# Attention scores from two-part fp32r operands on the array's two row halves, in place of three-part bf16 operands on 96 rows

## What is computed

```
q, k, v = split(x @ w)                      # layer 0: 32 heads of k and v; layer 1: 8, each for 4 heads of q
q, k = rope(q), rope(k)                     # 16 features a head
scores = q @ k^T / sqrt(16), causal         # 1024 x 1024 for each of 32 heads
attn = softmax(scores) ; y = attn @ v
```

## Time and profile before

| | us |
|---|---|
| median of 3 runs (1092.49 to 1099.5) | 1098.1 |
| span of the profiled execution | 1084.4 |
| PE busy, of it | 924.4 |
| DVE busy | 700.9 |
| ACT busy | 485.7 |
| POOL busy | 254.2 |
| mean granted TensorE clock, of full speed | 0.917 |

### The profile page before, as it was taken

One profiled execution on the slowest core, in us unless ns is written; L12 is line 12 of the kernel. 1 busy time (PEld: TensorE's weight loads), 2 busy tenths in 40 slices (PEclk: granted clock), 3 DMA queues, 4 the chain that ended last, 5 costly groups with the idle time before them and its releaser, 6 DMA issues. The chain is left out here.

```text
span 1084.4 us, 17334 instructions
## 1 busy us (share of the span) xinstructions
PE 924.4 (85%) x5462; PEld 512.0 (47%) x5462; DVE 700.9 (65%) x1305; ACT 485.7 (45%) x750; POOL 254.2 (23%) x397
## 2 busy tenths in 40 slices
PE   7879943789988898888977877999999988799998
PEld 5557821333333333257535532333444426677766
DVE  6975332668666766448584765988888835745564
ACT  4221401336544655642262213566666673346730
POOL 2554020022112111210614531221212223012300
PEclk9998965889889989999788977999999999999999
DMA  9221161112211321020001330011111101042001
GB/s 315 88 89 59 23 144 42 42 48 87 71 56 59 81 72 54 11 97 1 1 0 56 103 94 23 24 46 46 46 44 44 24 1 39 11 173 78 20 21 59
DMA packets 45537, 64.87 MB, mean 60 GB/s; under 512 B 9056, under 2 KB 32160, under 8 KB 43936
## 3 DMA queue, kind: packets, MB, share of 16 engines
q1 hardware_dynamic: 45472, 64.01, 19.7%
HBM read 51.27 MB, written 12.32 MB: 59 GB/s over the span
## 5 line engine op out<-in xcount | busy, mean ns | idle before, releaser
L1035 DVE TENSOR_REDUCE mx<-psum 128x1 f32<-128x512 f32 (+3 forms) x640 | 372.1, 632 | 157.9 <-PE psum L866 132.1
L980 ACT ACTIVATE arena_p<-psum 128x1024 f32<-128x1024 f32 (+3 forms) x384 | 294.0, 808 | 271.5 <-PE psum L883 270.7
L861 PE MATMUL psum<-arena_s 96*128 96x512 bf16 (+3 forms) x768 | 236.7, 349 | 53.8 <-DMA arena_s<-k_parts 43.4
L883 PE MATMUL psum<-arena_s 99*128 99x512 bf16 (+3 forms) x768 | 191.1, 340 | 30.3 <-DMA arena_s<-mT 26.7
L1098 POOL TENSOR_SCALAR_AFFINE_SELECT arena_p<-arena_p 128x256 f32<-128x256 f32 x256 | 102.8, 407 | 472.5 <-ACT arena_p L980 470.7
L903 PE MATMUL psum<-arena_p,v_grp 128*32 128x512 f32 (+3 forms) x1536 | 171.2, 519 | 2.1 <-POOL arena_p L1098 1.9
L861 PEld LDWEIGHTS psum<-arena_s 96*128 96x128 bf16 x768 | 77.5, 102 | 200.9 <-DVE mx L1035 107.4
L883 PEld LDWEIGHTS psum<-arena_s 99*128 99x128 bf16 x768 | 64.9, 100 | 94.9 <-ACT arena_p L980 23.4
L866 PE MATMUL psum<-maskb,ident_b 128*128 128x128 bf16 x512 | 109.1, 235 | 0.0
L255 PE MATMUL psum<-x_h,w 128*128 128x512 f32 x224 | 89.9, 465 | 10.4 <-DVE w L472 7.3
L866 PEld LDWEIGHTS psum<-maskb,ident_b 128*128 128x128 bf16 x512 | 54.1, 106 | 13.0 <-issue 1.6
(11 more groups left out here) (200 smaller groups left out, 1087.3 us busy)
## 6 DMA issues: line engine op xcount, KB each, us to landing
q_parts<-arena_p SPq DMA_DIRECT2D x48, 128.0 KB
arena_s<-q_parts SPq DMA_DIRECT2D x32, 192.0 KB, 3.0
arena_s<-k_parts SPq DMA_DIRECT2D x16, 384.0 KB
ff_raw<-in_w_in SPq DMA_DIRECT2D x11, 512.0 KB, 3.5
arena_s<-q_parts SPq DMA_DIRECT2D x32, 128.0 KB, 2.9
arena_s<-k_parts SPq DMA_DIRECT2D x16, 256.0 KB
k_parts<-arena_p SPq DMA_DIRECT2D x30, 128.0 KB
arena_w<-in_w SPq DMA_DIRECT2D x12, 256.0 KB, 6.5
```

Of the source, the lines that this page charges most:

```text
L861: last = pe.matmul(psum[:, bank, width * n:width * n + width], q_st[0:KS, s, c, 512 * r + P * i:512 * r + P * i + P], k_max[0:KS, s, T * k ...
L883: last = pe.matmul(psum[:, 2 * hp + h, o:512], k_exp[0:KM, s, T * kh + P * kt:T * kh + P * kt + P], q_st[0:KM, s, c, 512 * r + o:512 * r + ...
L980: act.activation(pr[:, n % NP_RING, :, o:512], psum[:, 2 * (b % 2):2 * (b % 2) + 2, o:512], ACT.Exp, scale=scale).then_inc(exp_ready, 1)
L1035: dve.tensor_reduce(mx[:, kc, col:col + 4 * len(heads) - 3:4], src, AX, ALU.max)\
```

## The change

q and k become two parts each in fp32r (4 bytes an element): high and the rest. q is stored as high, high, low and k as high, low, high, so one head's three products take 48 rows, with two rows of the maximum (50). Heads r = 0, 2 of a group lie on partitions 0 to 49, heads 1, 3 on 64 to 113, and two heads' scores are issued next to each other on the two row halves. One k buffer serves both jobs. Its constant -1 rows are in DRAM, stored once by SP in layer 0's projection.

The units run chunk by chunk: all eight short ones, then all eight long ones. The max pieces run two units ahead in place of one group. Buffers for q and k are four units deep, the first four units' loads are issued ahead (layer 0) or the first one's (layer 1). The maxima are split in two by POOL (`split_max`), and turned in fp32. The causal mask is two small bf16 matmuls on 64 rows, 128 and 64 columns wide, in place of one of 128. All loops are written out. In the projection POOL's and DVE's middle steps fall away, the parts have twice the bytes, and the order of units changes to chunk by chunk.

```diff
-
-PAIRS = [(0, 0), (1, 0), (2, 0), (0, 1), (1, 1), (0, 2)]
-KS = len(PAIRS) * D
-KM = KS + NPART
+KS = NPART * D
+KM = KS + 2
+NS = 4
 VW = 32
 ADP = 10
...
+    for c in range(CH):
+        both = [[("q", t, c) for t in range(KC)], [("k", t, c) for t in range(nk)]]
+        units += both[layer] + both[1 - layer]
 
...
+                                 parts[:, n % 2, part, :].bitcast(F32)).then_inc(stored[n % 2], 16)
+                if layer == 0 and n == 0:
+                    sp.wait_ge(consts, 7)
+                    for k_dst in m["k_parts"]:
+                        heads = k_dst.shape[0]
+                        for c in range(CH):
+                            sp.dma_start(k_dst[:, KS:KM, 512 * c:512 * c + 512], minus[0:2 * heads, :])\
+                                .then_inc(minus_stored, 16)
...
-                dve.wait_ge(mid_ready, n + 1)
-                dve.tensor_tensor(parts[:, n % 2, 2, :], t_cos[:, n % 2, :], parts[:, n % 2, 1, :],
+                dve.wait_ge(hi_ready, n + 1)
+                if n >= 2:
+                    dve.wait_ge(stored[n % 2], 16 * NPART * (n // 2))
+                dve.tensor_tensor(parts[:, n % 2, 1, :], rotated(n), parts[:, n % 2, 0, :].bitcast(F32),
                                   ALU.subtract).then_inc(lo_ready, 1)
 
             def cut_low(n):
...
-                pool.wait_ge(hi_ready, n + 1)
-                pool.tensor_tensor(t_cos[:, s, :], rotated(n), parts[:, s, 0, :], ALU.subtract)\
-                    .then_inc(res_ready, 1)
 
...
-
-
-    kr, q_st, k_max, k_exp = stacked.kr, stacked.q, stacked.k_max, stacked.k_exp
-    q_loaded, km_loaded, ke_loaded = stacked.q_loaded, stacked.km_loaded, stacked.ke_loaded
+    def load(self, sp, u):
+
+        c, g = divmod(u, NG)
+        s, n = u % NS, 512 * (c + 1)
+        for t in range(2):
+            sp.dma_start(self.q[64 * t:64 * t + KS, s, :, :].bitcast(F32),
+                         self.q_parts[g, t, :, :, 512 * c:n]).then_inc(self.q_loaded[s], 16)
+            if self.layer == 0:
...
-                sp.wait_ge(qk_taken, entry + 1)
-                for j in range(NPART):
-                    sp.dma_start(q_st[KS + j:KS + j + 1, s, c, :].rearrange("p (i t) -> p i t", t=P),
-                                 mT[R * 4 * j:R * 4 * (j + 1), c, :]).then_inc(max_loaded[s][c], 16)
+            def load_max(u):
+                s = u % NS
+                sp.wait_ge(qk_taken, turn_entry(u) + 1)
+                for t in range(2):
+                    for j in range(2):
+                        row = 64 * t + KS + j
+                        sp.dma_start(q_st[row:row + 1, s, :, :].bitcast(F32)
+                                     .rearrange("o p n -> o (p n)").rearrange("o (i q) -> o i q", q=P),
+                                     mT[16 * j + 8 * t:16 * j + 8 * t + 8, u % 2, :])\
+                            .then_inc(max_loaded[s], 16)
...
+            for u in range(stacked.first, NS):
+                stacked.load(sp, u)
+            load_max(0)
+            for u in range(NU):
+                if u + 1 < NU:
+                    load_max(u + 1)
+                if u + NS < NU:
+                    sp.wait_ge(scores_ready, first_exp[u + 1])
+                    stacked.load(sp, u + NS)
...
+                s, c = b % NS, steps[b][0]
+                if number == first_entry[b]:
+                    pe.wait_ge(q_loaded[s], 32 * (b // NS + 1))
+                    pe.wait_ge(k_loaded[s], 32 * (b // NS + 1))
                 for n, r in enumerate(heads):
-                    kh = r if layer == 0 else 0
-                    last = pe.matmul(psum[:, bank, width * n:width * n + width],
-                                     q_st[0:KS, s, c, 512 * r + P * i:512 * r + P * i + P],
-                                     k_max[0:KS, s, T * kh + 512 * kc:T * kh + 512 * kc + width],
+                    p, rows = r // 2, slice(64 * (r % 2), 64 * (r % 2) + KS)
+                    end = width * (n + 1)
+                    last = pe.matmul(psum[:, bank, width * n:end],
+                                     q_st[rows, s, p, P * i:P * i + P],
+                                     k_st[rows, s, key_pair(p), 512 * kc:512 * kc + width],
                                      start=True, stop=kc < c)
                     if kc == c:
-                        last = pe.matmul(psum[:, bank, width * (n + 1) - P:width * (n + 1)],
-                                         ident_b[:, :], maskb[:, :], start=False, stop=True)
+                        half = slice(64 * (r % 2), 64 * (r % 2) + 64)
+                        pe.matmul(psum[:, bank, end - P:end], picks[0][half, :], maskb[half, :],
+                                  start=False, stop=False)
+                        last = pe.matmul(psum[:, bank, end - 64:end], picks[1][half, :],
+                                         maskb[half, 0:64], start=False, stop=True)
                 last.then_inc(qk_ready, 1)
...
-                        pe.wait_ge(ke_loaded[s], 48 * pair + 48)
-                if not (isinstance(pair, int) and 2 * pair + s == 0 and n < 2):
-                    pe.wait_ge(exp_ready, BG * (2 * pair + s) + n - 1)
-                for h in range(2):
-                    r = 2 * hp + h
-                    kh = r if layer == 0 else 0
-                    last = pe.matmul(psum[:, 2 * hp + h, o:512],
-                                     k_exp[0:KM, s, T * kh + P * kt:T * kh + P * kt + P],
-                                     q_st[0:KM, s, c, 512 * r + o:512 * r + 512],
-                                     start=True, stop=True)
+                if kt == 0 and p == 0:
+                    pe.wait_ge(max_loaded[s], 64 * (u // NS + 1))
+                if n >= 2:
+                    pe.wait_ge(exp_ready, n - 1)
+                for t in range(2):
+                    rows = slice(64 * t, 64 * t + KM)
+                    last = pe.matmul(psum[:, 2 * (n % 2) + t, o:512],
+                                     k_st[rows, s, key_pair(p), P * kt:P * kt + P],
+                                     q_st[rows, s, p, o:512], start=True, stop=True)
                 last.then_inc(scores_ready, 1)
...
+            for b in range(2):
+                for n, what in enumerate(lists[b]):
+                    entry(first_entry[b] + n, b, what)
+            scores(0, 0, 0)
+            scores(0, 0, 1)
+            for u in range(NU):
+                c = steps[u][0]
+                todo = lists[u + 2] if u + 2 <= NU else []
+                n_slots = 4 * n_tiles[c]
+                issued = 0
+                for slot in range(n_slots):
+                    kt, part = divmod(slot, 4)
+                    ahead = (u, kt + 1) if kt + 1 < n_tiles[c] else (u + 1, 0)
+                    if part < 2 and ahead[0] < NU:
+                        scores(*ahead, part)
+                    if part == 3:
+                        values(u, kt)
+                    while issued < (len(todo) if u + 2 == NU else len(todo) * (slot + 1) // n_slots):
+                        entry(first_entry[u + 2] + issued, u + 2, todo[issued])
+                        issued += 1
...
+                    pool.wait_ge(max_joined, u - NG + 1)
+                else:
+                    pool.wait_ge(qk_taken, first_entry[u] + len(lists[u]))
+                if u >= 2:
+                    pool.wait_ge(qk_ready, turn_entry(u - 2) + 1)
+                pool.tensor_copy(high, m).then_inc(max_high, 1)
+                pool.wait_ge(max_high, u + 1)
+                pool.tensor_tensor(low, m, high.bitcast(F32), ALU.subtract).then_inc(max_ready, 1)
```

500 lines of the change are left out of this document (191 added, 309 removed).

## The result

The changed kernel takes 1127.4 us (median of 4 runs, 1121.65 to 1144.83), the kernel before 1095.3 beside it on the same chip (4 runs). The ratio is 1.029, with a 95% interval of 1.021 to 1.036: slower by 3%. The profiled execution has a span of 1119.9 us, against 1084.4 before, and a mean granted clock of 0.815 against 0.917. The prediction's span was 1008, so 112 us are to be accounted for. (In medians it is 105: the 13.7 us that the prediction kept between span and median lie for the most part not around the span. The changed kernel's profiled execution took 1121.8 us, 1.9 more than its span; the rest is spread between executions.)

What follows compares the result with a forecast made beforehand. Long units were bound by PE with DVE close behind, layer 0's start and short units by k loads. Layer 0 -72, layer 1 -12, projection +5, with caution -76: span 1008, plus 13.7 gives 1022 us; range 995 to 1080.

Steps and rivals of the forecast that it cites:

- With 3 for the slow clock at the start: 238: Each layer's attention: units of 57, 34.4, 115.8 and 27.6 us, plus 3 for the slow clock, sum to 238 us.
- Loads no longer starve layer 0: Layer 0's attention: PE waits for loads less than 5 us; rival that loads still starve it, 1046 to 1120 us, 12%.
- A short unit of 9.5 us: Attention: PE terms of 8.4 us plus friction give 9.5 us for each of six short units a layer.
- With long pieces 17.2: Attention: two short units a layer that carry long units' max pieces, bound by DVE, take 17.2 us each.
- A long unit of 19.3: Attention: PE terms of 17.9 us plus friction give 19.3 us a long unit, bounds 18.0 and 20.5.
- The rival that pieces use the halves too: Attention: neighbouring max pieces overlap on different halves, DVE sets 17.8 us a long unit, kernel 997 us; chance 12%.
- The friction between PE and DVE: Attention's long units: 0.8 us before the change, through the ring of three banks; DVE expected to push harder afterwards.
- Both attentions within 10 us of each other: Sign of being right: both layers' attentions take the same time within 10 us.
- 0.2 us a unit for changes between full-height and half-height work: Attention: by the rule that a tiling mode change drains the engine, 0.2 us a unit, some 5 us.
- The first piece near 142, first scores near 157: Layer 0's start: first attention piece near 142 us (bounds 139 and 151), first scores near 157; gain 25 us.
- Projection +5: Larger stores counted as even; last landing, small stores and layer 1's late loads cost 5 us, bounds -5 and +16.
- Slower by the diagonal pieces, 1176: Attention: diagonal pieces cost 0.66 us in place of 0.26, 6.4 us more in 24 units, kernel 1176 us; chance 8%.

Runs made afterwards that it cites:

- the kernel of 1051.4: Changed kernel plus bursts, four added matmuls a short unit, two selects moved ahead, one added matmul a piece of two long lists; 1051.4 us, timed again 1069.9.
- The pair with 128 and 64 rows: Changed kernel plus bursts and four added matmuls a short unit: 1072.8 us with the added matmuls on 128 rows, 1136.3 us with them on 64.

## Why the prediction was wrong

**The step that failed** is the clock, and it stood in no term: "With 3 for the slow clock at the start: 238". All cadences were taken from rows at 1.00, and the clock before was 0.91 and 0.97 in attention, so a full clock was carried over to work of another shape. The sum of 238 from first scores to last copy was 293 in layer 0 (170.3 to 463.5) and 291 in layer 1 (646.0 to 937.3): 55 and 53 us, less 4 that were allowed for in layer 0. That is 104 of the 112 us; the rest is 13 at layer 0's start and 4 between the two attentions, less 1 behind them and less the 5 and 3 that the sum allowed. What failed in the working is thus the two terms for short units: 6 x 9.5 ran as 15.3 each, and 2 x 17.2 as 22.6 and 23.8. The kernel with bursts and four matmuls a unit gives half of it back (54.6 us), and the number of rows of the added matmuls alone switches that on and off. So it is shown by experiment that the low clock costs this time; what makes the chip grant it is shown in part only. Part of the gain in layer 0 came through as forecast (30 us of waits gone), and the clock took it back.

The page TensorE: Matmul & The Clock Gate of the Trainium skill (Part 1: The HAM clock gate) says that the default is the low clock and that the unit which sets it goes by how busy TensorE has lately been. The traces agree on the default (0.55 at the start of attention before, where PE works for 12 of 31 us), and don't agree on busyness if that is what the profile counts: a busy share of 95 to 100% went with 0.50. No such case was among the rivals; it would have read "the clock stays at 1.2 GHz in the short units, 16 of them by 6 us, 1118".

**Point by point:**
- *Loads no longer starve layer 0:* right, 3.1 us of waits, and the number of engines as read.
- *A short unit of 9.5 us:* right at full clock (9.34 in one unit of the kernel with long units first), 15.3 as it ran. *With long pieces 17.2:* 22.6 and 23.8 as it ran; 17.5 once, in the kernel of 1051.4.
- *A long unit of 19.3:* 19.7, and 22.5 with full-height masks. The rival that pieces use the halves too was true in its mechanism, with PE's rows showing pieces beside scores, and not in its gain: the unit didn't reach 17.8. The friction between PE and DVE is what was underrated, or the pairs' overlap overrated; which of them was not separated.
- *Both attentions within 10 us of each other:* right, 293 and 291 us from first scores to last copy.
- *0.2 us a unit for changes between full-height and half-height work:* not measured by itself; the full-height masks above cost 0.17 us each where they stand among half-height work.
- *The first piece near 142, first scores near 157:* wrong by 10 and 13, and the piece also lies beyond the bound of 151. The loads were issued as fast as hoped, or faster (0.35 us each), but from 142.65, not from 129.6:

```profile
142.65 0.35 SPq L720 DMA_DIRECT2D q_st<-q_parts  x1
...
161.28 2.76 SPq L810 DMA_DIRECT2D q_st<-mT  x4
```

- *Projection +5:* too little, and put in the wrong place. The stores "counted as even" look to be the bound of layer 0's projection: from 60 to 70 us the DMA share is 0.51, eight engines, at 175 GB/s, where it was 0.33 at 96 before; ACT waits 28.5 us for stores between 60 and 100 us, where it waited 23.3; and the adapter, whose last v tile lets the loads go, starts at 105.96 against 97.02. TensorE begins the adapter at the low clock, behind a wait of 4.05 us, and its first 32 matmuls take 7.1 us in place of 3.8. So most of the 13 us at layer 0's start are probably stores and what followed them. This is read from two traces, and wasn't tested by a run.

```profile
60.00:70.00 10.00, 8.59 (x31) 5.46 (x31) 4.48 (x7) 2.21 (x4) 2.58 (x2) 1.00 0.51 175
```

- *Slower by the diagonal pieces, 1176:* not the cause. That rival had 6.4 us more in a unit even at full clock, and the unit of 9.34 us has no room for it. The result fell on that side by another mechanism.

What stays open: what exactly the chip weighs, and what lets the clock fall. The falls in short units told above stand at, or within 2 us behind, waits of PE of 0.89 to 2.19 us, and with two selects moved ahead, which took such waits away, there were none in short units without long pieces; but the one in layer 0 of the kernel with long units first had a wait of only 0.41, and no run takes the waits away from a kernel without added matmuls. The pair with 128 and 64 rows changes only the rows filled, and added half-height matmuls that ran beside the other half worked too; columns of the array, the data (the added operand is an identity) and the kind of number were not varied by themselves. Nor is it shown why layer 0 and layer 1 differ under the same filling.

## What to carry to other kernels

Splitting the array into halves so that two heads fit was no gain here, since the clock fell: check the granted clock in each stretch, not the busy share, and price narrow, half-height work at both levels before counting on either. Where a stage sits at 1.2 GHz with the engine busy, try a short full-height burst in a wait ahead of it, a few filling matmuls where it waits anyway, and look at the engine's waits just ahead of each fall; here a burst, two such matmuls a unit and one wait less took a unit from 15.3 to 9.3 us. And a full-height instruction between half-height ones that should overlap costs more than its columns say: 0.17 us net here, though it streamed 64 fewer.

## What was not expected of the hardware

- TensorE stayed at 0.50 for some 160 us in each layer (152 to 316 and 630 to 790) while busy 95% of the time, and with 50.00 of 50 us busy in the kernel with full-height masks.
- The same code ran at either level: an unfilled short unit took 9.34 us right behind long units and 15.2 two units later, and the one with half-height filling 18.1 in layer 0 and 11.0 in layer 1.
- Half the clock made a short unit 1.64 times as long (9.34 to 15.3 us) and not twice. At full clock PE has waits for other engines there (it is busy for 9.24 of 10 us), which is part of the reason.
- Adding 24 matmuls a unit on half the rows cost 2.8 us a unit at half clock; on all rows 11.2.
